# A layer pipeline on one core: the state-space mixer scanned by batch, half and state with whole-length scans, and a shortened expert routing

## The reference

```
dA  = exp(delta[..., None] * A)                       # per token, channel, state
dBu = delta[..., None] * Bm[:, :, None, :] * xc[..., None]
h_t = dA_t * h_(t-1) + dBu_t ;  y_t = sum over states of h_t * C_t
out = (y + xc * D) * silu(z) @ W_out
```

## Time and profile before

| what | us |
|---|---|
| median of 3 runs | 1855.57 (1854.29 to 1856.03) |
| the profiled execution's own time | 1850.95 |
| its span, first to last instruction | 1849.2 |
| PE busy, matmul | 1426.4 (77%) |
| DVE busy | 1194.7 (65%) |
| ACT busy | 911.2 (49%) |
| POOL busy | 789.9 (43%) |

### The profile page before, as it was taken

How to read it: one execution, slowest core, us unless ns; L and a number is a source line. 1 busy time by engine, 2 the same in 40 slices (tenths; PEclk the granted TensorE clock), 3 DMA queues, 4 the chain that set the end, 5 groups by cost and what they waited for, 6 DMA issues and landing times. The chain is left out here.

```text
span 1849.2 us, 26829 instructions
## 1 busy us (share of the span) xinstructions
PE 1426.4 (77%) x8265; PEld 917.1 (50%) x8265; DVE 1194.7 (65%) x2917; ACT 911.2 (49%) x1871; POOL 789.9 (43%) x565
## 2 busy tenths in 40 slices
PE   2789999999988999999868788883268637687746
PEld 2555555565665555555544555553246212232646
DVE  4666766666566666666648643676713799999524
ACT  2676666667636766666517332331021565545124
POOL 1456555555515555554610000001053059998153
PEclk9999999999999999999988767985579768989668
DMA  1000000000000000000000000006111213221212
GB/s 57 7 7 7 0 6 6 6 6 6 1 7 7 7 6 0 6 6 6 0 14 1 7 7 6 23 4 205 25 36 46 67 50 108 91 87 50 71 40 73
DMA packets 42755, 53.74 MB, mean 29 GB/s; under 512 B 8561, under 2 KB 30218, under 8 KB 42418
## 3 DMA queue, kind: packets, MB, share of 16 engines
q1 hardware_dynamic: 39922, 47.10, 8.3%
q0 software_dynamic: 2752, 5.65, 1.3%
HBM read 43.08 MB, written 9.26 MB: 28 GB/s over the span
## 5 line engine op out<-in xcount | busy, mean ns | idle before, releaser
L386 POOL TENSOR_TENSOR l0a_A<-l0a_A,l0a_share 128x1024 f32<-128x1024 f32 (+6 forms) x128 | 218.8, 1709 | 168.9 <-DVE l0a_share L960 168.8
L504 ACT ACTIVATE l0a_A<-l0a_ring,l0a_low 128x512 f32<-128x512 f32 (+3 forms) x384 | 217.9, 578 | 102.7 <-DVE l0a_low L953 84.7
L950 DVE TENSOR_REDUCE l0a_low_part<-l0a_ring 128x2 f32<-128x1024 f32 (+3 forms) x128 | 130.5, 1021 | 86.9 <-PE l0a_ring L690 85.9
L711 PE MATMUL l0a_tr<-main_ident,l0a_A 128*128 128x128 f32 x1152 | 163.8, 279 | 22.1 <-ACT l0a_E L515 8.8
L2921 PE MATMUL mx_ysum<-mx_hst,main_ident 128*128 128x512 f32 x256 | 135.1, 663 | 41.8 <-POOL mx_hst L3040 34.0
L711 PEld LDWEIGHTS l0a_tr<-main_ident,l0a_A 128*128 128x128 f32 x1152 | 130.8, 143 | 64.1 <-issue 52.4
L3055 POOL TENSOR_TENSOR mx_dBu<-mx_XI,mx_BB 128x1024 f32<-128x1024 f32 x64 | 139.6, 2208 | 48.0 <-DVE mx_DT L3095 48.0
L965 DVE COPY l0a_E<-l0a_tr 128x512 f32<-128x512 f32 (+1 forms) x160 | 101.7, 636 | 80.4 <-PE l0a_tr L711 80.4
L720 PE MATMUL l0a_agg<-l0a_E,l0a_F 128*64 128x512 f32 (+3 forms) x768 | 144.4, 498 | 1.6 <-DVE l0a_E L993 0.9
L720 PE MATMUL l0a_agg<-l0a_E,l0a_VH 128*64 128x512 f32 (+3 forms) x768 | 130.9, 489 | 11.2 <-issue 11.2
L3024 ACT ACTIVATE mx_dA<-mx_DT,mx_A 128x512 f32<-128x512 f32 x128 | 88.2, 690 | 95.8 <-DVE mx_hst L3143 95.8
(11 more groups left out here) (507 smaller groups left out, 3526.2 us busy)
## 6 DMA issues: line engine op xcount, KB each, us to landing
mx_BB<-mx_brows SPq DMA_DIRECT2D x32, 512.0 KB, 3.7
l0a_wp<-in_wqkv SPq DMA_DIRECT2D x17, 192.0 KB
moe_rows<-moe_XR SPq DMA_DIRECT2D x2, 1032.0 KB
moe_Wg<-in_f_wg SPq DMA_DIRECT2D x8, 256.0 KB, 5.8
moe_Wu<-in_f_wu SPq DMA_DIRECT2D x8, 256.0 KB, 5.9
moe_Wd<-in_f_wd SPq DMA_DIRECT2D x8, 256.0 KB, 6.1
moe_Y<-rt_zeros SPq DMA_DIRECT2D x2, 1024.0 KB, 11.1
e_back<-moe_Y SPq DMA_DIRECT2D x8, 256.0 KB
```

Source lines behind the costliest of these rows:

```text
L386: pool.tensor_tensor(a, a, spread(share[:, it, 0:heads], [P, heads, w]), ALU.mult).then_inc(shared, 1)
L504: act.activation(A[:, it % 3, h, c0:c0 + n], pair(k % 2)[:, h, 0:n], ACT.Exp, bias=low[:, it, h:h + 1], accum_out=s).then_inc(exp_done, 1)
L711: mm = pe.transpose(tr[n % 2][:, at:at + P], A[:, it % 3, h, t * P:(t + 1) * P], ident[:, :])
L950: dve.tensor_reduce(low_part[:, it - 4, :, r], src, AX_X, ALU.max, negate=True).then_inc(low_part_done, 1)
```

## The change

The mixer's pieces run over states fastest, then halves, then batches. Each piece has one scan of 1024 steps. The decays get two PSUM tiles, for which the second ysum tile is given up: one ysum serves all four sections of 16 pieces, and `finish` for a section stands behind scan 3 of the next. Rows of B and of C are loaded and spread for each piece, no longer for each two. ACT's copy of C of a pooled piece k-1 stands behind the exponential of piece k. POOL's product with silu(z) stands at piece 5 of the next section. In the routing, the copy of XR goes from POOL to ACT, the widening and the scans are done in four parts, the search computes `fresh`, T with the next digit, beside the vote, and the ranks are turned by transposes into the four banks wt, from which DVE reads every 16th column.

```diff
-        Cp, dA = pb("Cp", [P, SEQ]), pb("dA", [P, SEQ])
-        ysum = [pb(f"ysum{h}", [P, SEQ]) for h in range(HALF)]
+        Cp, ysum = pb("Cp", [P, SEQ]), pb("ysum", [P, SEQ])
+        dA = [pb(f"dA{n}", [P, SEQ]) for n in range(2)]
...
-            return k // HALF // NS, k // HALF % NS, k % HALF
-        on_pool = [k % HALF == 1 and k // HALF % 4 != 3 for k in range(PIECES)]
+            return k // NS // HALF, k % NS, k // NS % HALF
+        on_pool = [k % 8 in (1, 3, 5) for k in range(PIECES)]
... (SP)
-            for q in range(3, ROWS):
+            for q in range(3, PIECES):
                 b_row(q)
-                if q % 3 == 1 and q // 3 <= len(later[0]):
+                if q % 6 == 1 and q // 6 <= len(later[0]):
... (PE)
-                if n == 0 and b:
-                    pe.wait_ge(ysum_read, HALF * (b - 1) + h + 1)
+                if n == 0 and k:
+                    pe.wait_ge(ysum_read, k // NS)
...
+            def row_c(k):
+                b, n, h = piece(k)
+                if k:
+                    wait(pe, hc_dve, k - pooled[k])
+                    wait(pe, c_kept, pooled[k])
+                rows(Cp, n, b, c_ready)
             row_c(0)
             for k in range(PIECES):
                 if k >= 2:
                     state_sum(k - 2)
-                if k % HALF == HALF - 1 and k + 1 < PIECES:
-                    row_c(k // HALF + 1)
+                if k + 1 < PIECES:
+                    row_c(k + 1)
... (ACT)
+            def keep_c(k):
+                act.wait_ge(c_ready, k + 1)
+                if pooled[k] >= 2:
+                    act.wait_ge(hc_pool, pooled[k] - 1)
+                act.activation(CC[:, pooled[k] % 2, :], Cp[:, :], ACT.Copy).then_inc(c_kept, 1)
             for k in range(PIECES):
                 b, n, h = piece(k)
+                if k >= 2:
+                    act.wait_ge(scanned, k - 1)
+                act.activation(dA[k % 2][:, :], DT[:, h, seq(b)], ACT.Exp, scale=A[:, h, n:n + 1]).then_inc(dA_ready, 1)
+                if k and on_pool[k - 1]:
+                    keep_c(k - 1)
... (POOL)
-                if n == 3 and b:
-                    finish(b - 1, h)
+                if n == 5 and k >= NS:
+                    finish(*sections[k // NS - 1])
... (DVE)
+            for k in range(PIECES):
+                scan(k)
+                if k and not on_pool[k - 1]:
+                    weigh(k - 1)
+                if k % NS == 3 and k >= NS:
+                    finish(*sections[k // NS - 1])
+            weigh(PIECES - 1)
+            finish(NB - 1, HALF - 1)
... (routing: PE)
-            for half in range(2):
-                pe.wait_ge(pk_ready, half + 1)
-                for t in range(half * TT // 2, (half + 1) * TT // 2):
-                    mm = pe.matmul(pp[:, t, :], cum[:, t * P:(t + 1) * P], pickrow[:, :], start=True, stop=True)
+            for g in range(4):
+                pe.wait_ge(pk_ready, g + 1)
+                if g == 3:
+                    pe.transpose(lastp[:, :], cum[:, TOK - 1:TOK].broadcast_to([P, P]), ident[:, :])
+                for t in range(4):
+                    mm = pe.transpose(wt[g][:, t * P:(t + 1) * P], cum[:, (4 * g + t) * P:(4 * g + t + 1) * P], ident[:, :])
+                mm.then_inc(pp_ready, 1)
... (routing: DVE, the search, per digit k)
+                if k:
+                    step.then_wait(dve, dve.tensor_tensor(T[:, :], T[:, :], inc[:, :], ALU.bitwise_or))
+                if k + 1 < DIGITS:
+                    step.then_wait(dve, dve.tensor_tensor(fresh[:, :], T[:, :], digits[:, k + 1:k + 2], ALU.bitwise_or))
                 dve.wait_ge(votes_ready, k + 1)
                 step.then_wait(dve, dve.tensor_scalar(inc[:, :], votes[:, 0:1], 1.0, float(2 ** (28 - 4 * k)),
                                                       ALU.subtract, ALU.mult))
-                step.then_wait(dve, dve.tensor_tensor(T[:, :], T[:, :], inc[:, :], ALU.bitwise_or))
+                if k + 1 < DIGITS:
+                    step.then_wait(dve, dve.tensor_tensor(cand[:, :], fresh[:, :], inc[:, :], ALU.bitwise_or))
```

More of the change, by code:

```diff
@@ L1978, in l2_moe @@
         with ExitStack() as routing:
-            wr, prio, same, pickrow = (routing.enter_context(nc.sbuf_tensor("moe_" + n, [P, c], F32))
-                                       for n, c in (("wr", NE), ("prio", NE), ("same", P), ("pickrow", NE)))
+            wr, prio, same = (routing.enter_context(nc.sbuf_tensor("moe_" + n, [P, c], F32))
+                                for n, c in (("wr", NE), ("prio", NE), ("same", P)))
             digits = routing.enter_context(nc.sbuf_tensor("moe_digits", [P, 8], I32))
@@ L2001, in route_slots @@
         zeros = sb("zeros", [P, TOK])
-        T, cand, inc = sb("T", [P, 1], I32), sb("cand", [P, 1], I32), sb("inc", [P, 1], I32)
+        T, cand, inc, fresh = (sb(n, [P, 1], I32) for n in ("T", "cand", "inc", "fresh"))
         cnt, flag = sb("cnt", [P, 1]), sb("flag", [P, 1])
@@ L2156, in _ @@
             step.then_wait(dve, dve.scalar_tensor_tensor(keep[:, :], WR[:, :], cut, keep[:, :], ALU.is_equal, ALU.add))
[L2157 to L2161 removed]
+            for g in range(4):
+                if g:
+                    dve.wait_ge(pk_ready, g)
+                s = slice(g * 512, (g + 1) * 512)
+                dve.tensor_tensor_scan(cum[:, s], keep[:, s], zeros[:, s], cum[:, g * 512 - 1:g * 512] if g else 0.0,
+                                       ALU.add, ALU.add).then_inc(pk_ready, 1)
             dve.wait_ge(cut_ready, 1)
@@ L2165, in _ @@
             step.mark(dve.tensor_tensor(equal[:, :, :], prob[:, :, :], cuts, ALU.is_equal))
-            dve.wait_ge(pp_ready, 1)
-            step.mark(dve.tensor_copy(code[:, :, :], pp[:, :, :]))
+            for g in range(4):
+                dve.wait_ge(pp_ready, g + 1)
+                step.mark(dve.tensor_copy(code[:, 4 * g:4 * g + 4, :],
+                                          wt[g][:, :].rearrange("p (t e r) -> p t e r", t=4, e=NE)[:, :, :, 0]))
             step.mark(dve.tensor_copy(lastcode[:, :], lastp[:, 0:P:R]))
@@ L3062, in _ @@
                     weigh(k)
-            for h in range(HALF):
-                finish(NB - 1, h)
+            finish(NB - 1, HALF - 1)
         @block.vector
@@ new lines, in finish, with scan @@
+                dve.scalar_tensor_tensor(s, s, Dp[:, h:h + 1], ysum[:, :], ALU.mult, ALU.add).then_inc(ysum_read, 1)
+            def scan(k):
+                if k >= DEEP:
+                    dve.wait_ge(summed, k - DEEP + 1)
+                dve.wait_ge(dBu_ready, k + 1)
+                dve.wait_ge(dA_ready, k + 1)
+                dve.tensor_tensor_scan(hst[:, k % DEEP, :], dA[k % 2][:, :], dBu[:, k % DEEP, :], 0.0,
+                                       ALU.mult, ALU.add).then_inc(scanned, 1)
@@ L3146, in weigh @@
             def weigh(k):
-                dve.wait_ge(c_ready, k // HALF + 1)
-                if k % HALF == 0 and on_pool[k + 1]:
-                    dve.wait_ge(c_kept, pooled[k] + 1)
-                dve.wait_ge(scanned, k * 2 + 2)
+                dve.wait_ge(c_ready, k + 1)
+                dve.wait_ge(scanned, k + 1)
                 dve.tensor_tensor(hst[:, k % DEEP, :], hst[:, k % DEEP, :], Cp[:, :], ALU.mult).then_inc(hc_dve, 1)
-            for k in range(0, PIECES, HALF):
-                b, n, h = piece(k)
-                scan(k, 0)
-                scan(k, 1)
-                scan(k + 1, 0)
-                weigh(k)
-                scan(k + 1, 1)
-                if n == 1 and b:
-                    finish(b - 1, 0)
-                    finish(b - 1, 1)
-                if not on_pool[k + 1]:
-                    weigh(k + 1)
```

82 lines of the change are left out of this document (25 added, 57 removed).

## The result

The changed kernel takes **1877.52 us** (1872.96 to 1878.67, 4 runs) against 1854.93 (1850.51 to 1856.03, 4 runs) of the kernel before, run beside it: ratio 1.0115, 95% interval 1.0099 to 1.0131, or 22.6 us more. Forecast were 1870.5 within 1858 to 1884, and 15 us more than before. The profiled execution took 1876.89 us, its span is 1874.9, the mean granted clock 0.888.

The account below looks back on a forecast made before the run. It took DVE to bound the mixer, POOL 4% behind, and DVE's serial chain the routing. Mixer +22 and routing -7 gave +15: 1850.95 profiled became 1866, plus 4.6 for the median, 1870.5 us; range 1858 to 1884.

Parts of the forecast that it names:

- Scans: Mixer loop on DVE: one scan of 1024 replaces two of 512; alone worth 15 us, not to be had because of POOL.
- C path: Mixer: weigh k-1, row k on PE through one PSUM tile, ACT's copy, POOL's weigh; an 8.7 us chain with scans.
- Circle: Mixer loop: 8.7 us chain plus 17.6 us of POOL's work make 26.3 us per eight pieces, 1.25 more than before.
- First eight: First eight pieces of the mixer's loop: as before, 25.1 us, since POOL starts ahead.
- Borders: Three section borders in the loop: sum 16 waits for finish, row 19 for sum 16; 4.9 us each, plus 2.5 for PE's clock.
- Last eight: Last eight pieces: +1.25 us, some 2.3 more for late weigh 61 and its sums, minus 0.6 for the gate's product.
- Routing: Routing on DVE: copy of XR, widening in four, search and ranks together -7.0 us; bounds -5 to -8.5.
- copy and wide: Routing's start: copy of XR moved to ACT, -1.7 us; widening in four parts lets PE start earlier, -0.9.
- A dearer dBu with each new row of B: Rival 3, mixer: POOL pays 2.32 us for each dBu using a new B row; +7 us, 1877; 12%.
- rival 6: The mixer's loss is only as large as routing's gain: no change; 4%.
- 1, 2 and 4: 1: circle closes faster, 1842.5 us, 8%; 2: only routing counts, 1848.5, 4%; 4: PE's clock stays low, 1902, 7%.
- the circle closes faster: Rival 1, mixer: POOL's copy and weigh never wait for C, so POOL's 24.05 us sets the pace; 1842.5 us; 8%.

Follow-up runs that it names:

- both cures: Changed kernel with POOL weighing piece k-3 instead of k-2 and DVE's finish behind scan 2: 1823.72 us, ratio 0.9987 to the kernel before.
- other pieces: Changed kernel with POOL weighing k-3, finish behind scan 2, and POOL weighing pieces 2, 5, 6 instead of 1, 3, 5: 1818.20 us, ratio 0.9959.
- the last version: Changed kernel with k-3, finish behind scan 2, pooled pieces 2, 5, 6, XI rows 1032 wide, BB and CC 8 bytes in: 1815.14 us, ratio 0.9942.

## Why the prediction was right, and which terms were off

The direction, the range and both mechanisms held, though 15 us more were forecast and 22.6 measured; by the two profiles loop and routing together make 21.1, where 22 - 7 = 15 had been forecast. The wait of POOL on the copy of C is there at 2.7 to 2.8 us (2.3 forecast), goes when the copy doesn't wait, and shrinks when POOL weighs later; PE stands still at the borders for the finish, and an earlier finish takes most of that away. By its own steps:

- *Scans.* 2.29 as forecast, and their 15 us were not to be had. In the changed kernel the C path took them; with both cures, other pieces and shorter products on POOL the loop is 204.7 and plain eights 24.64 where DVE's own sum is 23.2: of the loop's 208.3 us 3.6 were won. What separates 24.64 from 23.2 is a term that the prediction put at nothing ("ACT loses its half-and-half exponentials: no path"): the exponential behind the copy of C costs DVE 0.74 us each time. In the changed kernel this limit, 25.4, lies just under the circle's 25.5 in the sections of cheap dBu, so the sum didn't show it. It is what caps the gain of a later weigh, and no run moved the exponential ahead of the copy.
- *Circle.* 26.3 forecast for each plain eight; 27.20, 25.54 and 25.90 measured, 78.64 against 78.9 in sum. The sum hides two errors. I had dBu at 2.14, a mean over two halves; the price goes by section. In sections 1 and 2 all cost 1.97, so circle and POOL's work are shorter (but the wait longer, 2.8): 8.7 + 3 x 2.31 + 5 x 1.97 = 25.5, which is what the eight in section 1 takes. The chain of 8.7 us measured 8.7 there, from the end of the first dBu behind 1589.45 to 1600.15.
- *First eight.* 25.1 forecast as "before", 26.55 measured. It is no exception from the circle: without the wait for C it takes 25.47, with the later weigh 24.81, both with the same dBu. Beside that, section 0 pays the dear price for every dBu, where before only one half did: 8 x 2.31 + 3 x 2.31 = 25.4 of POOL alone. POOL's timeline of after shows four in 9.32 us, and a product behind them:
```profile
1526.68 2.38 POOL L3052 TENSOR_TENSOR mx_hst<-mx_hst,mx_CC 128x1024 f32<-128x1024 f32 x1
1528.98 9.32 POOL L3066 TENSOR_TENSOR mx_dBu<-mx_XI,mx_BB 128x1024 f32<-128x1024 f32 x4
```
- *Borders.* This is the term that was mis-sized most. Forecast 3 x (26.3 + 4.9) + 2.5 = 96.1; measured 98.85. The walk from S (POOL's weigh 17, 1567.60) is right up to the finish: scan 19, weigh 18 and finish stand at S + 1.1, 3.3 and 4.4. Then sum 16 and row 19 take until the copy at S + 9.9 instead of 8.1: 3.15 us from sum 16 to row 19 instead of 1.88, and 0.93 instead of 0.6 for the row. PE had idled for 4.47 us and was slower afterwards, as in the earlier trace rows; I had priced this at 0.8 per border, here it is 1.8. POOL loses 4.76, not 2.6, also since its two dBu before were 0.35 cheaper than I had them.
- *Last eight.* From scan 56 to the last finish 31.76 against 27.23, +4.5; forecast +3.0. Section 3 is the other one with dear products: the three dBu after 1706.50 take 6.96.
- *Sum of the loop.* 204.04 from scan 0 to scan 56 against 181.06: +23.0 where 19.0 were forecast; with the end +27.5 where 22 were. Of the 5.5 that were missing, 1.45 lie in the first eight, 1.5 in the last and 2.75 at the borders; the plain circles give 0.25 back.
- *Routing.* -6.4 forecast -7.0. The first candidate stands 12.71 us after the start instead of 15.18 (-2.5, forecast -2.6 for copy and wide); from there to the end of the search (the first `keep`) it takes 29.65 instead of 30.42 (-0.8, forecast -1.15: T moved into the vote's shadow, its neighbours did not fit there fully); from there to `overs`, with the scans and the ranks, it takes 10.60 instead of 13.79 (-3.2 as forecast). What of it reaches the end is less sure: -3.9 in the run of it alone.
- *The lock.* L1565 takes 1.96 or 1.95 beside POOL's copy in two kernels and 0.29 beside ACT's in the third, and the copy's move costs 1.6 back when undone. The rule of the Trainium skill, SBUF — State Buffer, Who interferes with whom, that a DVE instruction with two SBUF inputs and a GpSimd instruction reading SBUF exclude each other while ACT doesn't wait, agrees with this.
- *Rivals.* A dearer dBu with each new row of B is ruled out: sections 1 and 2 load as many rows, at 1.97. The trace of before could have ruled it out too: there half 0 is the dear one in the first batch (2.36 us against 2.00 in the median), but in the second batch half 1, the second user of each row (2.35 against 2.00). But the rival was right in one point, that dBu's two prices matter for the sum; they go with the place of the data. The range leaves out rival 6 as well as 1, 2 and 4: no change would have been about 1855.6. That the circle closes faster did not come true; it decides at the C path, as said. PE's clock was granted 0.87 and 0.94 in the two windows shown below, with PE busy for 16.8 and 15.6 us of 26, so it was no bound.

One error is in first and last eight alike, beside C's path: I took a pair of unlike durations as a mean and did not ask what set them apart. What stays open: whether the experts' stretch and the front of the mixer give back some of the routing's gain, or only vary from one execution to the next; one profile of each kernel doesn't tell.

## What to carry to other kernels

Where a row in one PSUM buffer passes through several engines, add up the hand-offs from the release of that buffer to the product that needs it; if the engine that waits works in order, the work queued behind the wait pays, though every engine has time to spare. Place the in-order engine's item one step later, and put the instruction that frees a single buffer as early as its input allows: these two small moves were worth 24.9 us here, after a change whose own idea (fewer, longer scans) had left DVE with 7 us less to do and made the loop 27.5 longer. Then look for the next limit under the one that you cured: here an exponential queued behind the same copy on ACT. And when one instruction of fixed shape has two durations in a profile, find the cause before its mean goes into a sum.

## What the runs showed of the hardware

- POOL's product of two SBUF tiles, 128x1024 f32, comes every 1.97 us (it lasts 2.00) or every 2.31 (2.35), and it goes by where the data begin: cheap where one input begins 8 or 12 bytes past a multiple of 16 and the other input and the output at 0, dear at 0 and 4. Cheap were sections 2 and 1 of the changed kernel (12 and 8), and all of dBu and the weighings of the last version (8). Dear: sections 0 and 3 (0 and 4), and 16 bytes, which is 0 again; there two sections of one version took 2.41, which stays unexplained. The output's place was not varied.
- An instruction of DVE and one of POOL, both with two inputs in SBUF, slowed each other: beside POOL's first two dBu of the last version (2.90 and 2.97 us instead of 2.00) DVE's product for XI took 3.02 instead of 1.21.
- PE's sum of four matmuls takes 1.88 us right behind a row, and from its start to the next instruction 3.15 after PE had idled for 4.47 us at a border; before it was 3.75 after 7.78. In windows of the changed kernel the granted clock is 0.87 with a border and one idle stretch in it, 0.94 in another:
```profile
1557.00:1583.00 26.00, 16.84 (x36) 6.24 (x36) 19.91 (x12) 8.09 (x8) 18.13 (x9) 0.87 0.40 132
1609.00:1635.00 26.00, 15.63 (x39) 5.96 (x39) 21.18 (x14) 8.38 (x8) 20.14 (x10) 0.94 0.49 176
```
- The same kernel took 1856.41 us on one chip and 1824.91 on another; of the version with both cures and other pieces, profiled on the latter, experts and end took 93.5 and 115.9 us, where the kernel before has 101.5 and 135.9 in its own profile. Only ratios to a kernel run beside it on the same chip tell such changes apart.
